# Second attention of a two-layer decoder: one product of both heads with the values, in high and low parts, and the head scale moved into the output weights

## The reference, cut to what matters

```python
q = (x @ Wq).reshape(b, n, HEADS, DIM_HEAD).transpose(0, 2, 1, 3)
k = (x @ Wk).reshape(b, n, KV_HEADS, DIM_HEAD).transpose(0, 2, 1, 3)
v = (x @ Wv).reshape(b, n, KV_HEADS, DIM_HEAD).transpose(0, 2, 1, 3)
q = apply_rotary(q, cos, sin)
k = apply_rotary(k, cos, sin)
k = jnp.repeat(k, rep, axis=1)      # rep = 4
v = jnp.repeat(v, rep, axis=1)
scores = jnp.einsum('bhid,bhjd->bhij', q, k) * scale
scores = jnp.where(causal, scores, jnp.finfo(scores.dtype).min)
attn = jax.nn.softmax(scores, axis=-1)
out = jnp.einsum('bhij,bhjd->bhid', attn, v)
out = out * head_scale
out = out.transpose(0, 2, 1, 3).reshape(b, n, HEADS * DIM_HEAD)
return out @ Wo
```

## Time and profile before

| what | value |
|---|---|
| median of 3 runs | 903.34 us (898.98 to 904.95) |
| the profiled execution | 903.48 us, of it 901.7 us in the traced span |
| busy in the span | PE 801.8 us (89%), PEld 685.0 (76%), DVE 574.4 (64%), ACT 429.2 (48%), POOL 499.8 (55%) |
| second attention | from 435.9 to about 680 us of the span |

### The profile page before, as it was taken

The page is one execution under the profiler, slowest core; times in us unless marked ns, Lnnn a source line. Parts: engine busy times, 40 slices in busy tenths (PEclk is TensorE's granted clock), DMA queues, the critical chain, the costliest instruction groups (busy, mean ns, idle before and its releaser), DMA issues. The chain is left out here.

```text
span 901.7 us, 14551 instructions
## 1 busy us (share of the span) xinstructions
PE 801.8 (89%) x4733; PEld 685.0 (76%) x4733; DVE 574.4 (64%) x1651; ACT 429.2 (48%) x1209; POOL 499.8 (55%) x411
## 2 busy tenths in 40 slices
PE   7899999999999876792789999998987599999995
PEld 5678888888888764490678888887875388888885
DVE  4696867868769466123677667876736655545545
ACT  4264635536446544162366665666663532232232
POOL 4757287556587351513455564556422367777774
PEclk8999999999999997896999999999999799999998
DMA  6220711212315112553001111011001011111111
GB/s 200 71 94 1 234 36 59 94 36 106 115 50 180 55 54 65 186 120 88 30 6 48 53 53 53 1 54 53 24 1 37 12 35 52 35 52 52 35 41 47
DMA packets 58331, 59.09 MB, mean 66 GB/s; under 512 B 5392, under 2 KB 49312, under 8 KB 58272
## 3 DMA queue, kind: packets, MB, share of 16 engines
q1 hardware_dynamic: 57504, 56.24, 20.0%
q0 software_dynamic: 768, 2.10, 0.7%
HBM read 50.00 MB, written 8.32 MB: 65 GB/s over the span
## 5 line engine op out<-in xcount | busy, mean ns | idle before, releaser
L889 ACT ACTIVATE a_probs<-bank,a_neg_peak 128x128 f32<-128x128 f32 (+1 forms) x256 | 103.2, 429 | 88.9 <-DVE a_neg_peak L997 88.9
L917 ACT ACTIVATE a_probs<-a_probs,a_row_inv 128x128 f32<-128x128 f32 (+1 forms) x256 | 92.0, 447 | 20.8 <-DVE a_row_inv L1005 20.7
L997 DVE CUSTOM_DVE_ANT_0 bank<-bank,causal 128x128 f32<-128x128 f32 (+1 forms) x256 | 82.3, 394 | 15.3 <-PE bank L759 15.3
L895 ACT ACTIVATE a_probs_t<-bank 128x512 f32<-128x512 f32 x96 | 53.9, 597 | 73.5 <-PE bank L779 73.5
L1700 POOL TENSOR_TENSOR d_h_lo<-d_h,d_h_hi 128x512 fp32r<-128x512 f32 x40 | 51.7, 1293 | 52.6 <-ACT d_h_hi L1819 39.0
L398 POOL TENSOR_TENSOR a_wk_hi<-raw_k,one 128x512 fp32r<-128x512 f32 (+1 forms) x24 | 21.6, 901 | 102.3 <-DMA raw_k<-in_L_attn_w_k_dram 64.1
L798 PE MATMUL bank<-a_probs_t,a_vals 128*128 128x256 f32 x256 | 76.5, 380 | 0.0
L118 PE MATMUL bank<-a_wo_hi,a_ot_hi 128*128 128x256 f32 x256 | 74.5, 291 | 0.7 <-DVE a_ot_lo L1017 0.7
L1905 DVE TENSOR_TENSOR d_h<-d_silu,bank 128x512 f32<-128x512 f32 x40 | 27.5, 688 | 72.9 <-PE bank L120 72.8
L119 PE MATMUL bank<-a_wo_lo,a_ot_hi 128*128 128x256 f32 x256 | 73.2, 286 | 0.0
L120 PE MATMUL bank<-a_wo_hi,a_ot_lo 128*128 128x256 f32 x256 | 73.1, 286 | 0.0
(11 more groups left out here) (316 smaller groups left out, 2429.5 us busy)
## 6 DMA issues: line engine op xcount, KB each, us to landing
d_raw<-in_L_ffn_we_dram SPq DMA_DIRECT2D x48, 128.0 KB, 2.2
raw_k<-in_L_attn_w_k_dram SPq DMA_DIRECT2D x8, 512.0 KB, 6.5
raw_q<-in_L_attn_w_q_dram SPq DMA_DIRECT2D x8, 512.0 KB, 5.7
raw_v<-in_L_attn_w_v_dram SPq DMA_DIRECT2D x8, 512.0 KB, 7.3
raw_o<-in_L_attn_w_o_dram SPq DMA_DIRECT2D x8, 512.0 KB, 3.7
kv<-_L_ffn_expert_masks_dram SPq DMA_DIRECT2D x16, 256.0 KB, 3.1
kvt<-_L_ffn_expert_masks_dram SPq DMA_DIRECT2D x16, 256.0 KB, 3.1
raw_q<-in_L_attn_Wq_dram SPq DMA_DIRECT2D x8, 512.0 KB, 4.7
```

Source lines behind the costliest of these rows:

```text
L889: nc.scalar.activation(probs[s % 2][:, i, at:at + width], c.banks[i][:, at:at + width], ACT.Exp, bias=neg_peak[:, n:n + 1], scale=-1.0, ac ...
L895: nc.scalar.activation(probs_t[:, i * BANK:(i + 1) * BANK], c.banks[3 + (3 * s + i) % 2][:], ACT.Copy).then_inc(s_pt_free, 1)
L917: last = nc.scalar.activation(part, part, ACT.Copy, scale=row_inv[:, s % 2, n + r:n + r + 1])
L997: last = nc.vector.tensor_tensor_reduce(part, part, mask, -1.0, 3e38, ALU.add, ALU.min, neg_peak[:, n + r:n + r + 1])
```

## The change

Only the second attention (and the semaphores of the setup stage) is touched. The probabilities turned by TensorE are kept in a high and a low part: ScalarE's `pt` now writes the high part, and a new `turned_low` on VectorE subtracts it from the bank and writes the low part, and only this frees the bank. The values are kept in high and low parts as well (`first_values`, `second_values`). `pv` makes one `mm3` for both heads of a batch: the two heads share their value head, so the 512 columns of a bank are two heads of one batch instead of two batches of one head. It waits once for all three parts of the probabilities. The head scale no longer multiplies the attention output; GpSimd multiplies it into the raw output weights ahead of their split. `probs` moves into the memory of `c.spare`. The last output products wait bank by bank and are no longer cut between the third and fourth head. The setup's semaphores are cleared and released later on.

```diff
-        vals = [sb(f"vals{i}", [P, NT // 2, GROUP * DH]) for i in range(2 if rope else 1)]
-        probs = [sb(f"probs{i}", [P, 3, BANK]) for i in range(2)]
-        probs_t = sb("probs_t", [P, 3 * BANK])
+        if rope:
+            vals_hi, vals_lo = ([sb(f"vals_{n}{i}", [P, NT // 2, GROUP * DH], F32R) for i in range(2)] for n in ("hi", "lo"))
...
+            probs = [spare[:, i * 3 * BANK:(i + 1) * 3 * BANK].rearrange("p (r n) -> p r n", r=3) for i in range(2)]
...
+        probs_t = sb("probs_t", [P, 3 * BANK], F32R if rope else F32)
+        if rope:
+            probs_tl = sb("probs_tl", [P, 3 * BANK], F32R)
+            turned_hi, turned_lo = (ap[:].rearrange("p (j i n) -> p j i n", j=2, i=2) for ap in (probs_t, probs_tl))
...
                 def split_o(g):
+                    if rope:
+                        pool.wait_ge(weights.s_raw["o"], g * 16 + 16)
+                        scales = scale_row[:, g % GROUPS * GROUP:(g % GROUPS + 1) * GROUP].unsqueeze(2).broadcast_to([DH, GROUP, D])
+                        nc.gpsimd.tensor_tensor(weights.raw["o"], weights.raw["o"], scales, ALU.mult)
+                        pool.drain()
...
+                    if rope:
+                        cols, at = vals_cols(s, 0), s // PASS_STEPS
+                        pe.wait_ge(s_pt_free, 3 * s + 3)
+                        for i in range(2):
+                            bank = claim("pv", s, i)
+                            both = bank[:].rearrange("p (j t) -> p j t", j=2)
+                            for k, out, part in ((0, both, slice(0, T)), (1, both[:, :, P:], slice(T, T + P))):
+                                last = mm3(nc, out, vals_hi[at][:, 2 * i + k, cols], vals_lo[at][:, 2 * i + k, cols], turned_hi[:, :, i, part], turned_lo[:, :, i, part], k == 0, k == 1)
+                            last.then_inc(s_pv, 1)
+                        return
...
-                        nc.scalar.activation(probs_t[:, i * BANK:(i + 1) * BANK], c.banks[3 + (3 * s + i) % 2][:], ACT.Copy).then_inc(s_pt_free, 1)
+                        nc.scalar.activation(probs_t[:, i * BANK:(i + 1) * BANK], c.banks[3 + (3 * s + i) % 2][:], ACT.Copy).then_inc(s_pt_hi if rope else s_pt_free, 1)
...
-                            last = nc.scalar.activation(dst, src, ACT.Copy, scale=scale_row[:, head:head + 1])
+                            last = nc.scalar.activation(rows_of_batch(ot_hi, s, j), src.rearrange("p (j t) -> p j t", j=2), ACT.Copy)
...
+                def turned_low(s):
+
+                    for i in range(3):
+                        dve.wait_ge(s_pt_hi, 3 * s + i + 1)
+                        part = slice(i * BANK, (i + 1) * BANK)
+                        nc.vector.tensor_tensor(probs_tl[:, part], c.banks[3 + (3 * s + i) % 2][:], f32(probs_t[:, part]), ALU.subtract).then_inc(s_pt_free, 1)
...
                     if s < LAST:
                         peaks(s + 1)
+                    if rope:
+                        turned_low(s)
                     if not late:
                         for u in range(count):
                             proj(s + 2, u)
```

More of the change, by code:

```diff
@@ L558, in attention @@
         if rope:
[L559 removed]
+            s_turns, s_rope, s_pt_hi, s_vals_hi = S("turns"), S("rope"), S("pt_hi"), S("vals_hi")
         if not rope:
@@ L874, in _ @@
                         output(s // STEPS)
-                last_output(range(2, 3))
-                if not rope:
+                if rope:
+                    last_output(range(2, 4))
+                else:
+                    last_output(range(2, 3))
                     kept_transposes()
-                last_output(range(3, 4))
+                    last_output(range(3, 4))
             @block.scalar
@@ L929, in first_values, with second_values @@
                         act.wait_ge(s_v, t + 1)
-                        src = c.banks[3 + t % 2] if rope else ring_bank("v", 0, t)
-                        nc.scalar.activation(vals[0][:, t], src[:], ACT.Copy).then_inc(s_vals, 1)
+                        if rope:
+                            nc.scalar.activation(vals_hi[0][:, t], c.banks[3 + t % 2][:], ACT.Copy).then_inc(s_vals_hi, 1)
+                        else:
+                            nc.scalar.activation(vals[:, t], ring_bank("v", 0, t)[:], ACT.Copy).then_inc(s_vals, 1)
+                def second_values():
+                    for u in range(NT // 2):
+                        act.wait_ge(s_v, NT // 2 + u + 1)
+                        nc.scalar.activation(vals_hi[1][:, u], ring_bank("v", 1, u)[:], ACT.Copy).then_inc(s_vals_hi, 1)
                 if rope:
@@ L949, in _ @@
                     pv(s)
+                    if rope and s == PASS_STEPS - 2:
+                        second_values()
                     if s < LAST - 1 and late:
@@ L1071, in _ @@
                     proj(0, u)
+                if rope:
+                    first_values(range(0, 2))
                 peaks(0)
@@ L1075, in _ @@
                     threshold(NT - 1, u, u + 1)
+                if rope:
+                    first_values(range(2, NT // 2))
                 if not rope:
@@ L1609, in cross_and_experts @@
     OUT = NT // 2
+    for sem in c.finished:
+        nc.release_semaphore(sem)
     with ExitStack() as ctx:
```

58 lines of the change are left out of this document (42 added, 16 removed).

## The result

| kernel | median | runs | ratio to before (95% interval) |
|---|---|---|---|
| before | 904.14 us | 4 (898.98 to 905.39) | |
| after | 968.98 us | 4 (963.49 to 975.43) | 1.073 (1.065 to 1.081) |

A forecast was written before the change was run, and what follows sets the result against it. TensorE was taken to set the second attention's pace, with GpSimd's chain as long in odd steps. Even steps 46.9, odd steps 16.8 and last steps 2.2 gave 969.5 us; the falling clock's 10.5 made 980, range 958 to 1003.

The forecast's parts named there:

- The chain in front of the products: Second attention, every step: products wait for all three low parts, starting at 4.10 instead of 1.78 us, 2.32 us later.
- The even steps: Second attention: ropes queue behind VectorE's subtractions, delaying products and next scores; +6.7 us each, 46.9 us for seven.
- The products' saving: TensorE's products with the values: 2.10 us instead of 2.62, 0.51 us a step, swallowed in even steps by the rope wait.
- a quarter of 2.62: Products with the values: saving by the skill page's four passes against three, 0.65 us a step; prediction kept 0.51.
- The odd steps: Second attention: GpSimd's chain with the scale decides at full clock, +2.4 us each, 16.8 us for seven.
- The clock: Second attention: clock falls in nearly each even step; TensorE's odd step becomes 19.8 us, overtaking GpSimd; 10.5 us over seven.
- Start and end: Last two steps, without ropes: 2.2 us, bounds 0 and 3.6; at the start at most 1.4 us not under projections.
- the extra subtractions: Start of the second attention: four subtractions of 0.69 us, at most two of them, 1.4 us, not under projections.
- B: Second attention: the clock holds in most even steps; 960 to 972 us, most likely 969; chance 0.25.
- C: Second attention: clock low through most odd steps too, some 3 us more in seven pairs; about 1001 us; chance 0.08.
- D: Even steps: ropes do not gate, VectorE catches up; only the chain before the products stays, 33 us; 936 us; chance 0.07.
- E: Second attention: not slower, low parts lie wholly under TensorE's other work; 8.2 us gained, 895 us; chance 0.03.

The follow-up runs named there:

- The experiment with the chain alone: The kernel before, with whole fp32 products and no scale, plus VectorE's three subtractions into unused memory, gating banks and products: 973.95 us, ratio 1.078.
- fillers: The changed kernel with products on zeros added in TensorE's waits: in even steps alone 968.52 us, in the waits of both kinds of step 961.55 us.
- The two reordered kernels: The changed kernel with two ropes ahead of the low parts in even steps, 946.82 us; with projections, transposes, ropes, low parts alternating and the split moved, 930.07 us.

## Why the prediction was right, and where it was off

The forecast was 980 us with a range of 958 to 1003; 968.98 was measured, inside the range and 11 us below the likeliest value. Only about half of these 11 us lie in the steps. The forecast added 76.5 us and the traces show 70.7, of them 69.7 in the stage, with the odd steps 7.5 and the even ones 1.5 below the forecast, start and end 2.4 above. Nearly all the rest is that the profiled execution, from which the steps are read, is 6.5 us slower than the median of its four.

**The chain in front of the products: right.** Third transposes 2.02 us and products 4.08 us behind the first (481.48, 483.50, 485.56), foreseen 2.02 and 4.10. The experiment with the chain alone shows that, with what it pushes back behind it, it is enough for the whole loss.

**The even steps: right, in mechanism and size.** Foreseen +6.7 us each, 46.9; measured 45.4. The products stand at 6.17 and 8.23 us behind the first transposes, the scores at 11.68 (foreseen 6.2, 8.35, 11.8). The first was released by rope one and the last by the rotation, as named. For the second half the changed kernel can't tell rope two (over as the third rope starts, at 473.26) from TensorE's own pace, since the first half took 2.06 us at the low clock and not the 1.9 foreseen: its start at 473.31 is right behind both. With fillers and the full clock it started 8.20 us behind the transposes and waited for the rope there, so rope two would have held it in any case. The two reordered kernels confirm what delays the ropes.

**The products' saving: right that it vanishes.** 2.20 us for the twelve at full clock (485.56 to 487.76), foreseen 2.10, so they save 0.42 us and not 0.51; a quarter of 2.62, which the prediction weighed, would have left 1.97.

**The odd steps: the term was mis-sized.** Foreseen 16.8 at full clock and 10.5 for the clock, 27.3 in all; measured 19.8. The scale was taken at 2.4 us and is 2.03, so GpSimd's chain is 18.0 and not 18.3; that moves what is put down to the scale and what to the clock, but not their sum, which TensorE's list decides. Three sizes moved the sum. The scores behind an even step were taken at the low clock to their end, 5.1 us; the clock came back within them, and they took 4.72 in the first odd step (19.46) and 4.28 to 4.48 in five others (19.0 to 19.2). And step 7 has the projection of the values in front of it, comes at full clock, and took 17.68; I had charged the fall to all seven. Last, the other odd steps of before were counted at the 15.93 us of the first one; their mean is 16.1 (112.9 over 7), which takes 1.4 us off the difference. The choice of the decider held: TensorE's list with the fallen clock, not the scale, as the kernel without the scale shows. The clock is worth 7 us here, measured by the fillers placed in the waits (961.55; 6.9 in the odd steps), and not 10.5. Without the scale, where GpSimd's chain doesn't take over, the same fillers shorten the odd steps by 10.3 us in sum (132.7 to 122.4, in one execution each).

**Start and end: near.** The last stretch grew by 2.9 us (foreseen 2.2), and the start, from 437.01 to the scores of step 1 at 458.18, took 21.2 and not 19.5 us. These 1.65 us are not the extra subtractions for which the prediction had allowed up to 1.4: the wait for the low part of the values is 1.51 us, and the one for the copy of the values was 1.50. They are the clock at the first scores, as TensorE's timeline and a window of the changed kernel show:

```profile
446.53 1.88 PE L784 MATMUL bank<-a_keys,a_queries 128*128 128x128 f32 x8 [2.28 <-POOL a_queries L650]
448.00:450.00 2.00, 2.00 (x7) 1.64 (x7) 1.10 (x8) 0.41 (x3) 1.92 (x3) 0.50 0.00 0
```

The first score products took 1.88 us, and in the kernel without the scale 1.16 behind a wait of 2.29. From there to the scores of step 1 it is 11.65 us in the changed kernel's profiled execution, and 9.99 in the kernel before and in eight of the eleven kernels of the experiments, the one with the fillers in the waits, which has everything of the change, among them. So this part is the chance of one execution.

**The clock.** The term's premise is confirmed: 3.50 us of wait are followed by the granted clock 0.50. The Trainium skill, TensorE: Matmul & The Clock Gate, section HAM oscillation, says that waits between bursts of products make the clock fall and rise again and again; the trace agrees, with scores at the low clock behind six of the seven even steps. Fillers in the even steps alone left the time at 968.52, fillers in both brought it to 961.55.

Rivals: B (the clock holds, 969) has the measured number but not its mechanism, since the clock fell in nearly every pair; that the median landed on its 969 is chance, made of the sizes in the odd steps and of the distance between the profiled execution and the median. C, D and E are excluded by the steps.

## What to carry over

An operation that is put between a copy and the release of its bank is paid as often as the bank is awaited, and everything behind it in its engine's list moves too: here 0.69 us three times a step became 6.5 us, because the ropes stood behind it, with TensorE's rings and scores waiting for each. Before splitting an operand to save passes, put the saving (0.4 us a step) beside the length of the new chain (2.3 us) at a place where nothing else is queued for TensorE. And look where a side engine stands idle: moving the output weights' split there gave 0.5% on the kernel before (interval 0.2 to 0.7%), though GpSimd was busy for only 55% of the span.

## What the runs showed of the hardware

The low clock is not tied to the length of the hole in front of it. In the kernel without low parts it fell behind waits of 2.18 and 1.83 us for the rotation and held behind two of 1.99 and one of 1.95; in the kernel before it fell behind one wait of 3.40 us and held behind another. With the holes of the even steps filled, it fell behind waits of 0.98 and 1.41 us in the odd step, which stand in the changed kernel too and were followed there by full clock; the total stayed the same within 1 us. Behind nearly the same waits (3.41 and 3.50 us) it was back before the scores with fp32 products and not with fp32r ones. Which it is in a given step can't be told from the rows of that step alone, and executions of one kernel differ: those of the kernel with the chain alone had mean granted clocks from 0.920 to 0.932, and took 978.29 to 968.38 us. The multiplication of 128x1024 by a broadcast operand took 1.89 us on GpSimd, like the split's product with a broadcast one, and from its end to the next instruction, with the drain, it was 0.14.
